# Summing keys times values ahead of the key products, in pairs of tokens without a turn of weights

## The reference

```python
q = elu(x @ Wq + bq) + 1
k = elu(x @ Wk + bk) + 1
v = x @ Wv + bv
k = k / sqrt(sum(k * k, per head) + 1e-6)
attn = (q @ k.T) @ v            # per head and per batch row
y = layernorm(x + attn @ Wo + bo) * gamma + beta
x = layernorm(x + y)
out = layernorm(x + fp4_linear(silu(fp4_linear(x, w_gate)) * fp4_linear(x, w_up), w_down))
```

## Time and profile before

| what | value |
|---|---|
| median of 3 runs | 708.73 us (708.36 to 708.86) |
| the profiled execution, its own time | 708.65 us |
| its span, first to last instruction | 706.9 us |
| mean granted TensorE clock | 0.994 |
| instructions | 14230 |
| busy: PE, weight loads, DVE, ACT, POOL | 97%, 85%, 84%, 69%, 87% |

### The profile page before, as it was taken

One profiled execution on the slowest core, in us unless ns is written; L12 is line 12 of the kernel. 1 busy time (PEld: TensorE's weight loads), 2 busy tenths in 40 slices (PEclk: granted clock), 3 DMA queues, 4 the chain that ended last, 5 costly groups with the idle time before them and its releaser, 6 DMA issues.

```text
span 706.9 us, 14230 instructions
## 1 busy us (share of the span) xinstructions
PE 687.4 (97%) x4370; PEld 603.9 (85%) x4370; DVE 593.9 (84%) x1448; ACT 485.0 (69%) x943; POOL 611.9 (87%) x951
## 2 busy tenths in 40 slices
PE   7999999999988999999999999999999999999995
PEld 6887878778866799999999999999999999999995
DVE  5788888885878888898898898998998898998774
ACT  4666766766667767767767767767767767767664
POOL 2989888987998999988988988988988988989766
PEclk9999999999999999999999999999999999999999
DMA  9443343344322021111111111111111111100001
GB/s 280 170 136 134 128 135 123 113 165 152 118 91 90 30 62 45 61 46 46 56 65 46 60 46 46 53 68 46 61 46 46 52 69 46 60 17 16 16 32 45
DMA packets 22272, 55.05 MB, mean 78 GB/s; under 512 B 2547, under 2 KB 5557, under 8 KB 22197
## 3 DMA queue, kind: packets, MB, share of 16 engines
q1 hardware_dynamic: 21776, 54.01, 22.5%
q10 hardware_dynamic: 420, 0.13, 0.1%
HBM read 28.90 MB, written 25.17 MB: 76 GB/s over the span
## 4 chain that ended last, share of the span: by engine, by line
PE 89%; POOL 4%; issue 3%; DVE 2%; ACT 1%; DMA 1%; SPq 0%; POOLq 0%; DVEq 0%; ACTq 0%
PE banks L377 23%; PE banks L379 22%; PE banks L378 22%; PE banks L519 8%; PE banks L490 7%; PE banks L415 2%; PE banks L388 2%; PE banks L533 1%; PE banks L532 1%; PE banks L401 1%; PE banks L444 1%; DMA arena<-in_L_attn_x_dram 1%; POOL arena L1126 1%; PE banks L452 1%; POOL lnbuf L1111 0%
## 5 line engine op out<-in xcount | busy, mean ns | idle before, releaser
L377 PE MATMUL banks<-wgu_hi,actT_lo 128*128 128x512 f32 (+1 forms) x384 | 149.8, 390 | 1.6 <-DVE resid L790 1.3
L378 PE MATMUL banks<-wgu_lo,actT_hi 128*128 128x512 f32 (+1 forms) x384 | 144.0, 375 | 0.0
L379 PE MATMUL banks<-wgu_hi,actT_hi 128*128 128x512 f32 (+1 forms) x384 | 143.3, 373 | 0.0
L1126 POOL TENSOR_TENSOR arena<-arena 128x960 f32<-128x960 f16 (+2 forms) x68 | 115.1, 1693 | 0.0
L688 ACT ACTIVATE arena<-banks 128x512 f32<-128x512 f32 x64 | 38.4, 599 | 111.7 <-PE banks L379 111.5
L1102 POOL TENSOR_TENSOR arena<-arena 128x704 f32<-128x704 f32 x64 | 89.1, 1392 | 21.1 <-DVE arena L907 19.0
L377 PE MATMUL banks<-wd_hi,actT_lo 128*128 128x256 f32 x320 | 100.1, 313 | 0.0
L920 DVE TENSOR_TENSOR actT_lo<-banks,actT_hi 128x512 fp32r<-128x512 f32 (+1 forms) x132 | 85.6, 674 | 16.9 <-ACT actT_hi L674 16.2
L379 PE MATMUL banks<-wd_hi,actT_hi 128*128 128x256 f32 x320 | 90.3, 282 | 0.0
L378 PE MATMUL banks<-wd_lo,actT_hi 128*128 128x256 f32 x320 | 90.2, 282 | 0.0
L377 PEld LDWEIGHTS banks<-wgu_hi,actT_lo 128*128 128x128 f32 x384 | 72.5, 189 | 11.2 <-DVE resid L790 1.7
(11 more groups left out here) (126 smaller groups left out, 1932.8 us busy)
## 6 DMA issues: line engine op xcount, KB each, us to landing
xs<-x_plus_scratch SPq DMA_DIRECT2D x32, 512.0 KB, 3.3
x_plus_scratch<-xs SPq DMA_DIRECT2D x24, 512.0 KB, 2.9
arena<-in_L_attn_x_dram SPq DMA_DIRECT2D x32, 256.0 KB, 3.6
out_dram<-arena SPq DMA_DIRECT2D x32, 256.0 KB, 2.1
x_plus_scratch<-arena SPq DMA_DIRECT2D x8, 512.0 KB, 2.9
resid<-in_L_ffn_w_down_dram SPq DMA_DIRECT2D x1, 704.0 KB, 7.7
resid<-in_L_ffn_w_gate_dram SPq DMA_DIRECT2D x1, 640.0 KB, 8.1
resid<-in_L_ffn_w_up_dram SPq DMA_DIRECT2D x1, 640.0 KB, 9.5
```

Source lines behind the costliest of these rows:

```text
L377: nc.tensor.matmul(dst, sl, mh, start=(k == 0), stop=False, skip_group_check=shared)
L378: nc.tensor.matmul(dst, sh, ml, start=False, stop=False, skip_group_check=shared)
L379: last = nc.tensor.matmul(dst, sh, mh, start=False, stop=(ended and k == n - 1), skip_group_check=shared)
L1126: nc.gpsimd.tensor_tensor(blocks(va[:, (n + 1) % 2, a:b]), blocks(vqc[n % 2].bitcast(F16)[:, a:b]), each(s14[:, n % 2, a // BLK:b // BLK]) ...
```

## The change

In a step that has a pair p-2 and no turn of weights, the sum of keys times values is issued behind the turn of x and ahead of the key products. In the ten steps with a turn of weights it stays where it was, behind that turn. The same instructions with the same operands and waits are issued; nothing is added or removed, and no other engine's program changes.

```diff
                     x_transpose(p + 1)
+
+                if pair(p - 2) and p not in WG_STEP:
+                    kv_accumulate(p - 2)
                 if p == -1:
                     warm_up(6)
...
                 if p in WG_STEP:
                     pe.wait_ge(xT_lo_s, p + 2)
                     weights_turn(WG_STEP[p])
-                if pair(p - 2):
                     kv_accumulate(p - 2)
```

## The result

The changed kernel takes 722.88 us, median of 6 runs (721.03 to 725.61), against 708.62 us for the kernel before (707.27 to 708.92): a ratio of 1.0209, with a 95% interval of 1.0184 to 1.0234. It is slower by 14.3 us. I had said 2.7 us slower, so the sign was right and the size five times too small. The profiled execution took 725.08 us, 723.4 us of it span.

The account below looks back on a forecast made before the run. PE, busy 97% of the span, was taken as the bound, chiefly from 12 to 168 us. Waits of 0.9 + 1.2 + 0.6 = 2.7 us on 708.65 us gave 711.3 us; range 709.3 to 713.3 us.

Parts of the forecast that it names:

- First, A waits for k_hat: In step 2 the moved sum of keys times values (A) waits for the first normalised keys: 0.9 us lost.
- the keys are there, so no wait: In step 3 the keys are there at 24.20 us, the sum could not start before 25.1 us: no wait.
- A costs 0.81 us there and 0.84 us at the new place: PE time of the sum: 0.81 us behind the key products (K), 0.84 us behind the transposes; difference taken as zero.
- The rival of fp32 beside fp32: On PE, fp32 transposes beside the fp32 sum save entry time: 1.9 us faster, 706.8 us; faster outcome given 0.10.
- Step 2, 0.9 us: PE stands about 0.9 us ahead of the sum until the keys of pair 0 are written; not won back.
- The turns of weights, 4 x 0.3 us: In steps 8, 12, 16 and 18 POOL's dequantised chunk comes 0.3 us late for the turn of weights: 1.2 us.
- The tie of 0.01 us: DVE's L776 and POOL's L1022 start within 0.01 us; POOL was taken to win, making the chunk 0.3 us late.
- The sign that I had named, L452 waiting not at all: Ahead of the weight transposes: waiting 0.81 us or not at all, instead of about 0.3 us, would show the prediction wrong.
- Steps 19 to 22, 0.6 us: POOL's run 0.6 us later delays the keys for step 21 and the chunk for step 22: 0.6 us for both.
- From step 26 on, nothing: Edit costs nothing from step 26, since POOL takes the keys later than they could be had; without cover, 0.8 us once.
- A delay made early is found at the end: A delay made before 168 us is carried through the second stretch and the rest of the kernel to the end.

Follow-up runs that it names:

- The run with early masking: The changed kernel with every sum still moved, but DVE masks the heads of a finished batch row one step earlier: 710.62 us, ratio 1.0035.

## Why the prediction was wrong

**The step that failed** is "First, A waits for k_hat", which knows the keys as A's only late producer. I listed what the moved block waits for from two of its three waits, and the account of the code ahead of the prediction has only those two. The third, on kvt_s, stands in the code under `if p % PPB == 0`, so it holds for one sum in four. For every fourth step the argument "the keys are there, so no wait" was true and not enough. It made PE stand 11.6 us when those steps alone were moved, and the clock took some more on top; together 12.7 us of time. The run with early masking shows that this wait, and nothing else in the move, is the cause of that part. It could have been found from the trace of the kernel before: DVE's masking ends 0.15 us ahead of L415 in step 6, and 1.00, 0.96, 1.20 and 0.51 us ahead in steps 10, 14, 26 and 30. The move brings the sum forward by 3.0 us, and the 0.15 us between the two remain. So an estimate from these rows is 3.0 + 2.1 + 2.2 + 2.0 + 2.6 = 11.9 us of waiting. I read the distance between the last producer and the block for the keys, and not for the mask.

**"A costs 0.81 us there and 0.84 us at the new place"** was right to within 0.03 us. In the changed kernel, step 11:

```profile
81.44 0.60 PE L388 MATMUL banks<-ident,arena 128*128 128x128 f32 x4
81.97 0.69 PE L415 MATMUL banks<-arena 128*64 128x64 f32 x16
...
82.92 0.39 PE L378 MATMUL banks<-wkv_lo,actT_hi 128*128 128x512 f32 x1
```

From the first transpose to the second matmul of K it takes 1.48 us, 0.81 us more than the 0.67 us without A. The entry takes 0.53 us, against 0.55 predicted. The rival of fp32 beside fp32 is out: the block costs 0.81 us at both places.

**Step 2, 0.9 us:** right, 0.9 us. PE there (the view ends inside the group of the sum):

```profile
18.26 0.60 PE L388 MATMUL banks<-ident,arena 128*128 128x128 f32 x4
19.68 0.63 PE L415 MATMUL banks<-arena 128*64 128x64 f32 x14 [0.83 <-POOL arena L1051]
```

**The turns of weights, 4 x 0.3 us:** too much; 0.4 us in the changed kernel and 0.6 us when moved alone. The mechanism was the right one: against the turn of x, the chunk came 0.3, 0.1, 0.1 and 0.3 us late in steps 8, 12, 16 and 18 of the changed kernel, and 0.1, 0.2, 0.2 and 0.4 us late when those steps alone were moved. The tie of 0.01 us fell either way: in the changed kernel to POOL in step 7 and to DVE in 11 and 15, in the other to DVE in 7 and to POOL in 11 and 15. And where POOL won, about 0.1 us of the 0.2 to 0.3 reached the next turn of x. Only step 18, where POOL's instruction had already begun, paid its 0.2 to 0.4 us. The sign that I had named, L452 waiting not at all, is met in steps 12, 16 and 18, where PE is idle for under 0.05 us ahead of it.

**Steps 19 to 22, 0.6 us:** 0.3 us. The keys made PE wait 0.17 us in step 21 instead of 0.4, and the chunk of step 22 came 0.05 us late instead of 0.6.

**From step 26 on, nothing:** wrong, for the same missing wait: 2.0 us in step 26 of both kernels that moved its sum, and 2.0 us from step 30 in the changed kernel, where the clock was low for 6.8 us, but nothing there in the other. That POOL takes the keys late enough to cover PE's order holds for K's 0.81 us: with the first pairs left in place nothing is lost from step 26 on. It doesn't hold for a PE gap of 2 us in step 26. A reason would be that POOL itself works on what PE's turn of x sets off; no run tests it.

**A delay made early is found at the end:** right, in each trace within 0.2 us from the first gate activation to the last.

Without the missing term the sum would have been 0.9 + 0.4 + 0.3 = 1.6 us. The kernel in which the first pairs stay measures 2.3 us more than the run of before beside it, in medians, and 2.2 us in the spans of the profiled executions. So without the missing wait the forecast of 2.7 us would have looked right, in part by luck, since its terms measure only 1.6 us. That the 14.3 us have the forecast's sign says little for it.

## What to carry to other kernels

Before a block is moved forward in an in-order queue, write out every wait it issues, those under a condition too, and for each take from the trace how long its producer had been done when the block started. The smallest of these distances, not the one of the obvious producer, is how far the block can be moved without waiting; the list of waits can't show it, because a wait that is just met leaves no idle time.

A block belongs into a gap that exists. A sum that cost 3 us ahead of the key products in step 6 gave 0.7 us in step 22, where it went into a wait of PE.

## What the runs showed of the hardware

The same gap of 3 us in the same kernel was followed by PE's upper clock level in one execution and by 6.8 us at 1.2 GHz in another. In the four traces with moved first pairs, PE stands twelve times for DVE's masking, for 1.9 to 3.1 us. Behind the gaps of 2.1, 2.2, 2.8, 3.0 and 3.1 us the clock fell, for 3.4 or 6.8 us, at times before the gap had ended; behind those of 1.9, 1.9, 2.1, 2.2, 2.5, 2.9 and 2.9 us it did not. Within this range the length does not decide. That fits the wider spread of the changed kernel's times, 721.03 to 725.61 us against 707.27 to 708.92 us before: its two longest executions, 725.08 and 725.61 us, have mean granted clocks of 0.988 and 0.987, the other four 0.992 and 0.993.

A DVE rounding instruction of 0.26 us showed as 0.78, 0.98 and 1.24 us beside POOL's work, each time ending 0.1 us behind a POOL instruction; with POOL silent, 0.78 became 0.26 us. Its duration in a profile is then a date, not a price: the pair that started 0.8 us later ended 0.1 us later.
